# Residual rows of x: one plain transfer in SyncE's queue, or 28 indexed transfers issued by GpSimd

## The reference

```
h = inlayer2 @ W.T + b
f1 = h @ w1 + b1 ;  f2 = h @ w2 + b2
logits = f1[:, None] + f2[None, :]
bias_mat = NEG_BIG * (1.0 - (adj_mat > 0))
coefs = softmax(leaky_relu(logits, 0.01) + bias_mat)
x = x + coefs @ layernorm(x)                      # residual rows of x
x = x + ffn(layernorm(x))                         # top 2 of 8 experts, gelu, H = 256
```

## Time and profile before

| what | value |
|---|---|
| median of 2 runs | 578.06 us (578.05 to 578.07) |
| span of the profiled execution | 579.1 us |
| PE busy | 461.2 us (80%) |
| DVE busy | 476.2 us (82%) |
| ACT busy | 352.3 us (61%) |
| POOL busy | 101.3 us (17%) |
| moved by DMA | 94.83 MB, 164 GB/s over the span |

### The profile page before, as it was taken

How to read it: one execution, slowest core, us unless ns; L and a number is a source line. 1 busy time by engine, 2 the same in 40 slices (tenths; PEclk the granted TensorE clock), 3 DMA queues, 4 the chain that set the end, 5 groups by cost and what they waited for, 6 DMA issues and landing times.

```text
span 579.1 us, 6484 instructions
## 1 busy us (share of the span) xinstructions
PE 461.2 (80%) x1668; PEld 214.5 (37%) x1668; DVE 476.2 (82%) x726; ACT 352.3 (61%) x476; POOL 101.3 (17%) x73
## 2 busy tenths in 40 slices
PE   0620089793974896987999999997999999999996
PEld 0520053341431442442444434343443444444442
DVE  2679987773873879999999888967798989889885
ACT  0535087454453554664667574246989888888884
POOL 3916900410020009046020100101000000000000
PEclk9955579898998796896999999998999999999999
DMA  9999779999999999999899991025343356455321
GB/s 191 221 225 223 163 169 221 223 244 223 222 238 236 229 227 227 220 219 218 190 219 219 219 219 26 0 59 108 89 113 95 91 120 119 92 118 117 93 70 36
DMA packets 39954, 94.83 MB, mean 164 GB/s; under 512 B 5840, under 2 KB 11904, under 8 KB 39936
## 3 DMA queue, kind: packets, MB, share of 16 engines
q1 hardware_dynamic: 38688, 94.52, 74.6%
q10 hardware_dynamic: 1248, 0.10, 0.2%
HBM read 92.38 MB, written 2.23 MB: 163 GB/s over the span
## 4 chain that ended last, share of the span: by engine, by line
PE 33%; issue 21%; DVE 14%; DMA 12%; ACT 6%; POOL 1%; POOLq 1%; SPq 1%; DVEq 0%; ACTq 0%
DMA stage<-in_adj 10%; PE bank L1069 8%; DVE c L904 5%; PE bank L1114 4%; PE bank L1115 4%; PE bank L1116 4%; PE bank L1103 4%; PE bank L1104 4%; PE bank L1105 4%; DVE Y L766 3%; ACT mask L510 2%; DMA share<-shares 1%; ACT stage L628 1%; DVE maskT L942 1%; DVE stage L936 1%
## 5 line engine op out<-in xcount | busy, mean ns | idle before, releaser
L1069 PE MATMUL bank<-c,Y 128*128 128x512 f32 x512 | 247.6, 631 | 25.6 <-DVE c L904 24.1
L904 DVE SCALAR_TENSOR_TENSOR c<-g_row,r_col,maskT 128x512 f32<-128x512 uint8 (+1 forms) x256 | 202.3, 825 | 9.5 <-PE bank L1069 7.3
L510 ACT ACTIVATE mask<-stage,sig_bias 128x2048 uint8<-128x2048 int32 x59 | 117.6, 1999 | 84.7 <-DMA stage<-in_adj 61.4
L1069 PEld LDWEIGHTS bank<-c,Y 128*128 128x128 f32 x512 | 96.4, 199 | 158.1 <-DVE c L904 78.1
L628 ACT ACTIVATE stage<-bank,b1T 128x512 f32<-128x512 f32 x128 | 83.7, 687 | 23.1 <-PE bank L1105 21.5
L936 DVE TENSOR_TENSOR stage<-stage,share 128x1024 f32<-128x1024 f32 x64 | 78.3, 1223 | 21.4 <-ACT stage L628 14.9
L942 DVE TENSOR_TENSOR maskT<-stage,maskT 128x1024 f16<-128x1024 f32 x64 | 78.4, 1225 | 0.0
L707 DVE STREAM_TRANSPOSE maskT<-mask 128x512 uint32<-128x512 uint32 x64 | 45.0, 705 | 38.0 <-ACT mask L510 37.3
L635 ACT ACTIVATE maskT<-stage 128x1024 f16<-128x1024 f32 x64 | 67.3, 1052 | 3.4 <-DVE stage L936 3.3
L1114 PE MATMUL bank<-maskT,w2h 128*128 128x512 f16 x128 | 48.9, 382 | 5.8 <-DVE maskT L942 5.3
L1115 PE MATMUL bank<-maskT,w2h 128*128 128x512 f16 x128 | 49.0, 383 | 0.0
(11 more groups left out here) (152 smaller groups left out, 430.8 us busy)
## 6 DMA issues: line engine op xcount, KB each, us to landing
stage<-in_adj SPq DMA_DIRECT2D x256, 256.0 KB, 12.4
share<-shares SPq DMA_DIRECT2D x16, 1024.0 KB, 8.1
share<-in_L_gnn_inlayer SPq DMA_DIRECT2D x8, 256.0 KB, 6.7
share<-in_x SPq DMA_DIRECT2D x4, 512.0 KB, 16.1
out<-c SPq DMA_DIRECT2D x8, 256.0 KB, 3.9
share<-in_L_ffn_W SPq DMA_DIRECT2D x1, 1024.0 KB, 17.8
x<-in_x SPq DMA_DIRECT2D x1, 256.0 KB, 9.2
W_sb<-in_L_gnn_W ACTq DMA_DIRECT2D x1, 64.0 KB, 3.8
```

What stands on the lines that cost most here:

```text
L510: act.activation(mask[:, p % 2], stage[:, p % SLOTS], ACT.Sigmoid, bias=sig_bias[:], scale=1000.0).then_inc(conv_done, 1)
L904: dve.scalar_tensor_tensor(c[:, k % CR].rearrange("p (s i) -> p s i", i=32), g_row[:, bass.ds(s * ST, ST)].rearrange("p (s i) -> p s i", i ...
L1069: mm(bank[:, par, :], Y[:, k], c[:, k % CR], start=(k == 0), stop=(k == NK - 1)).then_inc(c_used, 1)
```

## The change

GpSimd makes a table `row_id` with `row_id[p, n] = 128 n + p` in the prologue. The one transfer of blocks 4 to 31 leaves SyncE's list. In its place GpSimd issues 28 indexed transfers, one for each block, ahead of `post(0)`; each takes its 128 row numbers of x from a column of `row_id` and brings 64 KB. They all raise `xn_in[1]`, and the wait ahead of `post(1)` is for 16 * 28 in place of 16. Blocks 0 to 3 come as before.

```diff
+        row_id = sb("row_id", [P, NK], U32)
...
             load_half(1, 1)
             load_half(2, 0)
-            sp.dma_start(x2[:, TS:NK], x_rows[:, TS:NK]).then_inc(xn_in[1], 16)
             load_half(2, 1)
...
+            pool.iota(row_id[:], [[P, NK]], base=0, channel_multiplier=1)
             pool.wait_ge(pool_step, 4)
...
+            for n in range(TS, NK):
+                pool.indirect_dma_start(x2[:, n], None, x, bass.IndirectOffsetOnAxis(row_id[:, n:n + 1], 0)).then_inc(xn_in[1], 16)
             pool.wait_ge(xn_in[0], 16)
             post(0)
-            pool.wait_ge(xn_in[1], 16)
+            pool.wait_ge(xn_in[1], 16 * (NK - TS))
             post(1)
```

## The result

| what | before | after |
|---|---|---|
| median of the runs | 578.06 us | 589.4 us (589.06 to 589.74, 2 runs) |
| ratio to before, 95% interval | | 1.0185 [1.0142, 1.0227] |
| span of the profiled execution | 579.1 us | 588.0 us (its own time: 589.74) |

A repetition beside the experiments gave 1.0178 [1.0131, 1.0225], 10.3 us [7.6, 13.0] more. The kernel became slower, by just under 2%. The forecast was 582.2 us, with a range of 573 to 607. Single runs of the kernel before lie between 575.5 and 581.4 us, and the profile shown of it belongs to one of the slower ones: wherever an execution has both, its time is 1.7 to 1.8 us above its span (589.74 and 588.0 here, 590.44 and 588.7, 570.04 and 568.3), so by that estimate it took about 580.8 us. This would explain why the spans of the two profiles differ by 8.9 us only, the medians by 11.3, and the repetition by 10.3.

What follows compares the result with a forecast made beforehand. DMA bytes bound the first 350 us; 28 gathers at 1.3 us (36.4) make xs late, so new bytes come at 157.3 against queued bytes' end at 153.2: +4.1 us on the 578.06 median, 582.2 us, range 573 to 607.

Steps and rivals of the forecast that it cites:

- the likeliest case: Forecast case: price of one gather from 1.15 to 1.57 us, time 578 to 590 us, chance 0.40.
- c: GpSimd's time for one indexed transfer, taken as two busy passes of 0.63 us, rounded up to 1.3 us.
- the signs of being wrong: Issue spacing under 1.15 or over 1.57 us; hole length unlike added time; rate during gathers well above 223 GB/s.
- 111.2 + 28c + 0.60 + 1.39: Moment GpSimd writes xs of tile 0: gathers from 111.2, then post(0)'s copy and 1.39 us add; forecast 149.6.
- Queued bytes last until 153.2: DMA queue during tile 0's stall: pieces waiting, one refilled and x rows feed the engines until 153.2 us, as before.
- The gain g: Gain from moving the transfer to GpSimd's queue, if gathered rows fill DMA waits: 0 to 7.4 us, taken as 0.
- 56 us of transfers that don't overlap: Skill's fixed 2.0 us per GpSimd DMA: 28 without overlap take 56 us, +24; but they should overlap.
- Rival A: GpSimd's issuing is cheap or hidden, c under 1.15: nothing stalls, 571 to 578 us; chance 0.25.
- Rival B: GpSimd becomes the bound, over 2% slower, at VectorE's wait for tile 0's xs; c from 1.57; chance 0.31.
- GpSimd's pass doubles when VectorE works beside it: Support for Rival B: a GpSimd pass over 128 or 129 columns takes 0.29 us alone, 0.63 beside busy VectorE.
- 3100 ns for a transfer issued by GpSimd beside a VectorE copy: Skill's figure, lists blocked by VectorE's two-port operation: 28 such transfers give +54 us; about 620 ns alone gives no stall.
- Rival C: Gathered rows arrive late for post(1)'s add; costs only once tile 1's xs is over 18.9 us late; alone 0.04.

Runs made afterwards that it cites:

- the busy kernel: 32 copies of 128x1024 on GpSimd ahead of post(0), no gathers, plain transfer kept in SyncE's queue, against the kernel before: 588.3 us, 1.0169.

## Why the prediction was right, and where its terms were off

**The mechanism** went as written: gathers ahead of post(0), xs late, VectorE, then ScalarE, then SyncE standing, and DMA running dry. The copies in place of gathers show that nothing else is needed for it. The direction was right, the 589.4 us lie in the range and inside the 578 to 590 of the likeliest case, at its upper edge. The amount was 4.1 us against 10.3 to 11.3 measured; three terms were mis-sized. That the time still fell into that case is partly luck: its width was meant for c alone, and c was nearly right, while most of the miss came from two terms that had no width at all. Of the signs of being wrong that it names, none came: the spacing was 1.33 on average, the hole has the length of the added time, and while gathers ran with VectorE idle the rate was 234 GB/s (239 over the same 125 to 145 us before, with the plain transfer in it).

**c.** 1.3 was taken, 1.33 measured: 28c is 37.2 and not 36.4, 0.8 us. The two passes of GpSimd from which it was made came out right by size, but not for the reason given (a list for every row): a plain transfer of 28 times as many rows took 1.87 us, so it is not rows as such that cost; what a gather pays for, the instruction or the indexed rows, is not shown.

**The way from the gathers to xs.** "111.2 + 28c + 0.60 + 1.39" has no room for the drain between the copy and the add. It was free before, and I read it as free. Measured 3.45 us in the timeline (4.23 in the repetition), and 3.8 us of time in the kernel without that drain. This is the step that was missed: an instruction that is not in the diff, but whose wait widens because of what the diff queues ahead of it.

**The end of the queued bytes.** "Queued bytes last until 153.2" took the moment at which ScalarE got p = 7 for the moment at which the engines had nothing left. They ran dry near 149.3. In the kernel before, more had been moved by 153.2 than all up to p = 7. By the windows from 110 us on it is 15 us at 221 GB/s, 20 at 239 and 8.2 at 224, together 9.9 MB; in the changed kernel, up to the hole, 15 at 232, 20 at 234, 4 at 230 and 3 at 25, together 9.2 MB. Counted from the start of the span it is 32.32 MB by 153.2, against 31.62 MB at the hole. The 0.7 to 0.8 MB between them are 3.1 to 3.5 us at 223 GB/s. The reading that fits is that p = 7 was complete only when much of the next piece had moved too; no run takes that apart. The copies of the busy kernel, with the plain transfer in place, show an end near 148.5 with the same 31.62 MB, so it is not a gain of the other queue. Against this, the first bytes moved at 160.2, 1.0 us after the mask instead of 1.98, and everything ran 0.3 us earlier.

Together: 4.1 + 0.8 + 3.45 - 1.0 - 0.3 + 3.9 = 10.95 us, for a hole of 11.1 in the windows and 10.3 [7.6, 13.0] in the runs. The terms are read from the trace that shows the hole, so only the agreement with the runs is a test of them. Against the profile of before the adds of GpSimd are later by 27.0 us at tile 0, 11.7 at tile 1 (182.16), 9.7 at tile 2 and 9.0 at tile 6; in the repetition it is 12.6 at tile 1 and 9.8 at tile 6. Whether the 2.7 us between 11.7 and 9.0 are won back in the changed kernel or lost in the slower execution of before can't be told with one profile of before, and stays open.

**The gain g.** I set it to 0 and kept 7.4 as the end. The gathers behind post(0), half of them ahead and the plain transfer from GpSimd, all with DMA full, gave 1.0034, 1.0005 and 0.9990: no gain by another queue was measured. The Trainium skill, DMA: Bandwidth & Descriptors, "Issuing engines are not separate DMA queues", says that all issuers run on the same 16 engines and that a second one saves only its sequencer's time; these runs agree with it.

**The fixed cost of one transfer.** Of the 2.0 us for one DMA issued by GpSimd (the Trainium skill, DMA: Bandwidth & Descriptors, "Anatomy of one DMA — SWDGE (gpsimd) path") the runs show nothing serial: transfers were issued every 1.26 us and landed 8.2 us later by the median of the profile's list, overlapping. The prediction's 56 us of transfers that don't overlap did not come about.

**Rival A** needed c under 1.15; the smallest spacing was 1.25. **Rival B** was decided from 11.6 us on, which the change missed by a hair; the place is B's, the price c is not (1.33, where B needed 1.57). As for its support, "GpSimd's pass doubles when VectorE works beside it": the gathers took 0.95 us with VectorE still and 0.95 to 1.52 with it busy, and VectorE stops at 125.6 by the very stall, so only those up to then could pay. But it would not have doubled otherwise either: behind post(0), with VectorE at work, the spacing was 1.33 us on average against 1.26. Of the 3100 ns for a transfer issued by GpSimd beside a VectorE copy (the Trainium skill, SBUF — State Buffer, "A bandwidth-pool intuition that's wrong (but worth ruling out)") nothing shows here; no run puts a gather beside such a copy on purpose, so none tests it. **Rival C** came about in the experiment with the gathers behind post(0): late rows, and at most the 2 us there as loss. The iota took 0.16 us at 2.83 and cost nothing.

## What to carry to other kernels

Count what stands behind an inserted instruction on its in-order engine, up to the first result that another engine waits for, and in that count the drains too: on GpSimd here they waited for its own transfers. In a stage bound by DMA, lateness of an engine is free up to what the buffers hold (here some 16 us: 12.8 us late cost nothing, and 10.3 us were lost with xs 26.8 us late) and costs nearly its full length beyond. And this transfer, in a full queue, was paid for whichever of the two engines issued it; look for the place where the DMA engines are idle, which here was worth 6 us, and 9 with all blocks there.

## What the runs showed of the hardware

- An indexed transfer of 128 rows took GpSimd 0.95 us, 1.26 from start to start, with VectorE idle. With VectorE at work single ones took up to 1.52, and the spacing was 1.33 on average (23 of them behind post(0)). One plain transfer of 3584 rows took it 1.87 us, against 0.89 for SyncE.
- A drain on GpSimd behind transfers that it issued itself held it until they had landed: 3.45 us behind the gathers, 21.57 behind the plain transfer, none when a semaphore of the copy took its place. It can hold longer: 1.3 us past the landing in the changed kernel, and with all gathers behind post(0) 2.46 us of idle time between the copy and the add of post(1), after all of them had landed. What that is stays open.
- The first gather behind post(0) was preceded by 8.75 us of idle time when no gather had run before, and by 0.80 when 14 or 22 had. Ahead of post(0) the first one had 0.19. I have no run that tells why.
- TensorE's granted clock fell to 0.50, the 1.2 GHz level, while it idled, and read 0.58 over 156 to 160 us, which it was busy throughout, and 1.00 over 160 to 164. Between 156 and 160.2 VectorE waited 0.28 and 0.16 us for it; the DMA engines were what the stage waited for, so I count it as nothing, though no run tests that.
